# A two-layer transformer kernel: TensorE waits for its own gate/up semaphore in every block of expert tokens

## The reference, cut to what matters

```
x = L0_attn_x
xn = _layernorm(x, axis=-1)
x = x + _L0_attn_ref(xn, ...) + _L0_ffn_ref(xn, ...)
xn = _layernorm(x, axis=-1)
x = x + _L1_attn_ref(xn, ...) + _L1_ffn_ref(xn, ...)

# _L1_ffn_ref: 64 experts, each token goes to 8 of them (by sigmoid scores, in groups)
def step(out, ws):
    wg, wu, wd, we = ws                       # 176 x 256, 176 x 256, 256 x 176, weight per token
    inter = jax.nn.silu(x @ wg.T) * (x @ wu.T)
    return (out + inter @ wd.T * we[:, None], None)
out, _ = jax.lax.scan(step, jnp.zeros_like(x), (gate_proj, up_proj, down_proj, w_full.T))
```

## Time and profile before

| | us |
|---|---|
| median of 3 runs | 1284.01 |
| lowest and highest run | 1283.94 and 1292.42 |
| span of the profiled execution | 1284.5 |
| PE busy in it | 1134.1 |
| DVE busy | 710.9 |
| ACT busy | 644.7 |
| POOL busy | 452.0 |

### The profile page before, as it was taken

The page is one execution under the profiler, slowest core; times in us unless marked ns, Lnnn a source line. Parts: engine busy times, 40 slices in busy tenths (PEclk is TensorE's granted clock), DMA queues, the critical chain, the costliest instruction groups (busy, mean ns, idle before and its releaser), DMA issues. The chain is left out here.

```text
span 1284.5 us, 25387 instructions
## 1 busy us (share of the span) xinstructions
PE 1134.1 (88%) x7606; PEld 655.4 (51%) x7606; DVE 710.9 (55%) x2605; ACT 644.7 (50%) x1340; POOL 452.0 (35%) x525
## 2 busy tenths in 40 slices
PE   7679999999999999988976898888888888888985
PEld 3356666666666666555543444444444444444464
DVE  6486565656566666322684544554444454454557
ACT  4215554545555454643364565556555655565620
POOL 3323132222220000013103556555565655565410
PEclk9799999999999999989888999999999999999997
DMA  7401131121112011100056536525374335655257
GB/s 230 86 10 29 22 54 28 29 37 39 29 28 47 20 21 20 52 17 33 22 153 128 172 110 201 162 88 186 110 217 134 122 106 165 199 156 190 74 210 301
DMA packets 81681, 129.67 MB, mean 101 GB/s; under 512 B 32776, under 2 KB 53001, under 8 KB 81034
## 3 DMA queue, kind: packets, MB, share of 16 engines
q1 hardware_dynamic: 61576, 76.94, 21.6%
q0 software_dynamic: 15360, 47.21, 11.8%
q10 hardware_dynamic: 4616, 3.91, 1.0%
HBM read 97.57 MB, written 30.05 MB: 99 GB/s over the span
## 5 line engine op out<-in xcount | busy, mean ns | idle before, releaser
L684 DVE CUSTOM_DVE_ANT_0 a_masked<-a_ps_s,a_mask 128x512 bf16<-128x512 f32 (+3 forms) x512 | 230.0, 487 | 159.3 <-PE a_ps_s L843 155.4
L600 ACT ACTIVATE a_probs<-a_ps_e 128x512 f32<-128x512 f32 (+1 forms) x384 | 188.2, 526 | 121.7 <-PE a_ps_e L863 120.6
L1865 PE MATMUL e_ps_y<-e_w_d,e_hT 88*64 x640 | 168.6, 386 | 69.7 <-DVE e_hT L1741 62.8
L1842 PE MATMUL e_ps_gu<-e_w_gu,e_xT 128*64 x640 | 227.5, 479 | 1.0 <-ACT e_s_gu L1668 1.0
L1842 PE MATMUL e_ps_gu<-e_s_gu,e_xT 128*64 128x352 f32 x640 | 227.5, 479 | 0.0
L1635 POOL DMA_INDIRECT y<-e_y,dst x160 | 159.6, 998 | 177.0 <-DVE e_pick L1724 98.8
L189 POOL DMA_INDIRECT yn<-rows,inv x160 | 157.1, 982 | 115.7 <-DVE inv L1404 61.4
L1733 DVE TENSOR_TENSOR e_h<-e_sg,e_ps_gu 128x176 f32<-128x176 f32 x160 | 54.0, 337 | 229.3 <-ACT e_sg L1650 143.7
L1865 PE MATMUL e_ps_y<-e_s_d,e_hT 88*64 88x256 f32 x640 | 169.0, 386 | 0.0
L1865 PEld LDWEIGHTS e_ps_y<-e_w_d,e_hT 88*64 88x64 f32 x640 | 80.8, 136 | 165.8 <-issue 141.8
L843 PE MATMUL a_ps_s<-a_kT,a_qT 72*128 72x512 bf16 (+3 forms) x512 | 131.3, 300 | 12.9 <-DVE a_headmax L684 11.2
(11 more groups left out here) (243 smaller groups left out, 1899.0 us busy)
## 6 DMA issues: line engine op xcount, KB each, us to landing
e_w_gu<-e_gu SPq DMA_DIRECT2D x64, 352.0 KB
e_w_d<-e_down SPq DMA_DIRECT2D x64, 176.0 KB
a_qT<-qk_parts SPq DMA_DIRECT2D x48, 192.0 KB
e_w_gu<-y SPq DMA_DIRECT2D x12, 768.0 KB, 6.2
qk_parts<-a_stage SPq DMA_DIRECT2D x16, 256.0 KB, 2.6
e_w_gu<-y SPq DMA_DIRECT2D x4, 1024.0 KB, 7.0
qkv<-y SPq DMA_DIRECT2D x12, 256.0 KB
yn<-rows,inv POOLq DMA_INDIRECT x160
```

The costliest lines, as they stand in the source:

```text
L600: nc.scalar.activation(probs[:, i % HKV, UCOL[u]:UCOL[u + 1]], ps_e[:, (i * 3 + u) % 2, 0:w], ACT.Exp, scale=SCALE0).then_inc(exp_done, 1)
L684: ins = V.tensor_tensor_reduce(masked[:, n % 2, c:c + w], ps_s[:, n % 2, c:c + w], mask[:, T - w:T], 1.0, -3e38, ALU.add, ALU.max, headmax ...
L1842: ins = nc.tensor.matmul(ps_gu[r * SEG:(r + 1) * SEG, j % 2, 0:2 * INTER1], xT[:, j % 2, k * P + r * SEG:k * P + (r + 1) * SEG], w.rearran ...
L1865: ins = nc.tensor.matmul(ps_y[r * SEG:(r + 1) * SEG, 0:D], hT[:, j % 2, k * P + r * SEG:k * P + (r + 1) * SEG], w.rearrange("p a d -> p (a ...
```

## The change

Two lines are added in TensorE's loop over the blocks. Behind `gate_up(j)` and `down(j - 2)` TensorE now waits until `gu_ready` counts j + 1, which is the increment of the last matmul of its own `gate_up(j)`.

```diff
                 if j >= 2:
                     down(j - 2, oldest)
+                if j < NBLK:
+                    pe.wait_ge(gu_ready, j + 1)
                 if j + 1 < NBLK:
                     after = expert_of(j + 1)
                 if j + 2 < NBLK:
                     transpose_x(j + 2)
                 if 1 <= j <= NBLK:
                     transpose_h(j - 1)
```

## The result

| | us |
|---|---|
| before, median of 4 runs | 1283.97 |
| changed, median of 4 runs | 1301.20 |
| changed, lowest and highest run | 1296.87 and 1304.61 |
| ratio, 95% interval | 1.0128, 1.0090 to 1.0166 |
| span of the profiled execution, changed | 1297.1 |

The change costs 17 us. It is slower, as forecast, but by less than a third of the +59 that the sum gave; the time lies inside the range (1208 to 1410).

The account below looks back on a forecast made before the run. TensorE was taken to bound the experts' stage, losing time to late gate/up semaphores. Standing for them +133 us, less 74 of breaks before down, gave +59: 1343 us forecast for the median, range 1208 to 1410.

Parts of the forecast that it names:

- the sum: Experts' stage, 160 blocks: TensorE standing for late gate/up semaphores +133 us, breaks before down saved -74, net +59.
- what bounds: Experts' stage: TensorE, busy 470 of 542 us, losing about 74 us to late products because gate/up's semaphore is seen late.
- the way the gain and the loss exchange: Per block, a TensorE stall of about 0.95 us before down is exchanged for one of up to 2.07 at the load.
- a prompt semaphore: Gate/up's update comes on time: down's own 0.9 us hides the added wait, costing 0 to 0.05 us a block.
- The forecast that I derived from it, no loss: From the skill's page: gate/up's update follows promptly, down covers the wait in each block, kernel stays at 1284.5 us.
- a held semaphore: Gate/up's update comes late and TensorE stands at the number's load: 55 times 2.07 us and 23 times 0.81, 133 us.
- The argument that their number would rather rise: With no breaks before down, every block is of the kind held now: above 78 late ones, at most 160; 78 kept.
- the third rival: Late update comes out once TensorE runs empty after down: 0.96 us lost in 78 blocks, about 1285 us; chance 0.20.
- what is given back: Silu, product and copies catch up while TensorE stands, so the 74 us of breaks before down go to nearly nothing.
- the clock: Longer breaks lower TensorE's granted clock: at 0.74 over the stage up to 157 us more, 1500 us; chance 0.05.
- The point of no change: Number of late gate/up semaphores at which TensorE's standing equals the 74 us of saved breaks: 43 of the assumed mix.
- The cured rival: TensorE running ahead causes the lateness, so the wait cures it: blocks of 2.79 us, 1214 us (1205 to 1230); chance 0.29.

Follow-up runs that it names:

- without late news: Kernel before, unchanged, in measurements where gate/up's semaphore reaches ScalarE promptly: 1198 to 1201 us; the changed kernel there 1205.6, ratio 1.0038.
- runs with lateness by hand: Kernel before and changed kernel, ScalarE loading registers before silu in 80 of 160 blocks; changed TensorE waits for ScalarE's count there: 1294.8 to 1463.9 us.
- four loads: Either kernel, ScalarE loading a register four times before silu in 80 blocks, silu 2.20 us late: before 1327.9, changed 1454.1 us (1427.9, 1463.9 in another measurement).
- two loads: Either kernel, ScalarE loading a register twice before silu in 80 blocks, silu 1.15 us late: changed 1294.8 (earlier 1322.4), before 1334.6 (earlier 1330.9) us.

## Why the prediction was right or wrong

**Right: what bounds, and the way the gain and the loss exchange.** The semaphore was late and not the work (the trace records gate/up's updates more than 0.3 us after the end of its last matmul 69 times of 150 in the kernel before, and never of 160 in the same kernel without late news), the breaks before down went away (68 to 13), and TensorE stood at the load instead. The runs with lateness by hand show each price of the sum: 2.17 us of standing for 2.20 of lateness (the sum would have 2.20 + 0.80 - 0.79 = 2.21), 1.08 for 1.15 (1.16).

**Right: a prompt semaphore.** 0 to 0.05 us a block was said, 0.03 at most was measured. There down's own work covers the wait; between gate/up and down, without that cover, it costs 0.41. The Trainium skill's page Perfetto Trace Analysis (section Per-instruction lifecycle, Tensor Engine Instruction) has PSUM acknowledge the write and push the update. It gives no times for that, so "no long delay" is my reading of it. The measurements without late news agree with this reading (silu's waits of 0.28 us), the others don't. The forecast that I derived from it, no loss, holds without late news to within 5 us; but there is nothing to give back then, and the kernel takes 1200 us and not 1284.5.

**Wrong: the term "a held semaphore", by its size.** The sum had 55 x 2.07 + 23 x 0.81 = 133 us, 1.70 for each of 78 blocks. The step that failed is the one that took number and lateness of the kernel before (78, 55 of them by 2.06 us) as givens of the chip that the change leaves alone. In the changed kernel silu starts more than 0.3 us late in 64 blocks, 35 times by 1.94 us in the mean and 29 times by 0.91. Measured as the sum has it, from the end of gate/up to the transposition less 0.79, TensorE loses 85 us in them. The profile divides that standing: 59.9 us in 61 waits before the transposition, and most of the 20.1 us before down, for the news of the transposed product comes late too ("DVE e_hT <- remote"). The price for a given lateness was right, as the runs by hand show. What was wrong is that the long ones would stay: about 55 became 35, and of the recorded updates of gate/up's semaphore 57 of 150 are over 1.2 us late in the kernel before, 29 of 124 in the changed one. The argument that their number would rather rise pointed the wrong way.

Of the two blocks above, the first looks like the third rival (out 0.22 us after TensorE ran empty, a loss of 0.98 where 0.96 was worked out), the second does not (0.85 after). But the first is not it either: down's own update, of a matmul that ended at 907.66, is recorded only at 908.64, when TensorE had long stood idle. In this block TensorE's running empty did not let down's news out. The third rival, to which I had given 0.20, has the size of half of the losses right, and not their cause.

The runs with lateness by hand say the same more strongly, here compared across measurements. With four loads, the kernel before takes 1427.9 with late news of its own and 1327.9 without, 100 us apart. The changed kernel takes 1463.9 and 1454.1, 10 us apart, and has next to no waits but those made by hand (4.0 us in the three left over). With two loads it is 1322.4 and 1294.8, 28 apart; with none, 1301.2 and 1205.6, 96. The recorded updates of gate/up's semaphore, all in measurements with late news, go the same way (some records are missing in each, of 160):

| kernel | recorded | over 0.3 us late |
|---|---|---|
| before | 150 | 69 |
| before, two loads | 152 and 144 | 68 and 60 |
| before, four loads | 144 | 50 |
| changed | 124 | 49 |
| changed, two loads | 105 | 14 |
| changed, four loads | 118 | 5 |
| before, without gathers | 121 | 2 |

The more TensorE stands by the change, the less there is of late news of the chip's own. That it is the standing that does it, and not the spacing of gathers which goes with it, was not separated.

**Roughly right: what is given back.** 74 us were said. The breaks behind a late product fall from 62.8 to 9.4 us, 53.4 recorded and 63 with 55 x 0.17 hidden. Against it stand new waits of down put to issue, 10.5 us in 18 (1.6 before). Of the 20.1 us that are left before down, 18.9 lie in the 64 blocks with late news, so they are part of the standing counted above, and beside it the 74 are given back nearly whole.

**Missing from the sum: the clock.** I had it as a rival at 0.05, with the whole stage at 0.74. It came in small: 0.96 in place of 0.99, 7.6 + 1.6 = 9 us. With longer breaks by hand it was 0.88 and 54 us, about as much as the waits themselves. But the mean break does not fix it: with two loads by hand TensorE stood 1.08 us in 77 waits at a clock of 1.00, longer and more often than the 0.98 in 61 that go with 0.96. What tells these apart was not found; the longest break is 1.9 us in the one and 2.9 in the other.

Summed again by the sum's own measure: standing +85, breaks -74, clock +9, together +20, against +12.6 between the profiled spans and +17 between the medians. As the profile divides it: +60, -63, +9 before down, +9 clock, together +15.

**Count.** The point of no change was put at 73 us of standing. 85 were measured, and the kernel is a little slower.

**The cured rival** (0.29) falls for this kernel: 27 "remote" waits of silu are left, and the time rose. But part of its idea may be true, as the runs by hand suggest: a TensorE that stands often has its news on time. The standing costs more than it saves.

## What to carry to other kernels

A wait put into a stream costs what the awaited thing is late, less the work in front of the wait: 0.40 us a block with none, 0.03 at most behind down, 0 within error behind the transpositions. A lateness that is read off one kernel may not be carried into the changed one as a constant where its cause is unknown: give its number and its size a range of their own. And give the clock a term of its own: here breaks of about 1 us cost 0 and 9 us, breaks of 2.17 us 54. Before a gain is read off one pair of measurements, measure the kernel before again: here the pair gave a ratio of 1.013 in one measurement and 1.004 in another.

## What the runs showed of the hardware that I had not expected

The same kernel takes about 1200 us in one measurement and 1284 to 1296 in another, on one core, and each kind repeats. The difference goes with TensorE's semaphore updates, which come up to 3.4 us late in the experts' stage: 69 of 150 recorded ones of gate/up are over 0.3 us late at 1284.5, and at 1194.4 all 160 are there within 0.03 us. The hold is not on one semaphore. All four of TensorE's are late (gate/up 69 of 150, the transposition of x 71 of 148, that of the product 83 of 110, down 70 of 140), and held updates come out together, 0.04 to 0.09 us apart in the block of the earlier trace rows.

Whether it goes with the chip or with the circumstances of the measurement is not settled; the record has chip number 0 once without late news (1199.6) and once with it (1285.9), so if the number names the same chip, the chip alone does not decide. It went away without the indirect gathers in the one run that could show it (1197.8 where 1285.9 was measured with them), and a TensorE that stands often is hardly touched by it (10 us between the kinds in place of 100). The way from a gather to TensorE's update is open.
